# Retention in a four-layer language model tower: the next pair's work placed between a pair's masks, with a second query buffer

## The reference, cut to what matters

```
q, k, v = x @ W_Q, x @ W_K, x @ W_V              # each (B, T, H, 16)
scores  = (q . k) / 4 * decay                    # causal, decay = gamma_h ** (t - s)
out     = scores @ v
normed  = (out - mean) / sqrt(var + 1e-5) * weight + bias      # by head
y       = silu(x @ W_G + normed) @ W_O
```

## Time and profile before

| | us |
|---|---|
| median of three runs | 2263.53 |
| the profiled execution | 2263.48 |
| its span, first to last instruction | 2261.7 |
| retention, four pairs: first scores to the last residual sum (389.74 to 573.12) | 183.4 |
| TensorE busy over the span | 1845.4 |
| VectorE busy over the span | 1746.0 |
| ScalarE busy over the span | 1316.9 |

### The profile page before, as it was taken

The page is one execution under the profiler, slowest core; times in us unless marked ns, Lnnn a source line. Parts: engine busy times, 40 slices in busy tenths (PEclk is TensorE's granted clock), DMA queues, the critical chain, the costliest instruction groups (busy, mean ns, idle before and its releaser), DMA issues. The chain is left out here.

```text
span 2261.7 us, 31852 instructions
## 1 busy us (share of the span) xinstructions
PE 1845.4 (82%) x11804; PEld 950.2 (42%) x11804; DVE 1746.0 (77%) x4911; ACT 1316.9 (58%) x1459; POOL 328.4 (15%) x392
## 2 busy tenths in 40 slices
PE   6999998988766678999899998889999889755930
PEld 3566655766421123344333443333443364333520
DVE  3676557667777789999999999999999889785532
ACT  1222222231226999999999999999999822110410
POOL 6000111010343000000000000000000000057256
PEclk9898998787778899999999999999999999877965
DMA  5501000000001100000000000000000000031732
GB/s 167 182 1 38 18 1 14 1 1 1 1 0 36 66 1 1 1 1 1 1 1 1 1 1 1 1 1 1 1 1 1 1 1 1 0 140 52 229 106 75
DMA packets 39658, 64.98 MB, mean 29 GB/s; under 512 B 7744, under 2 KB 27728, under 8 KB 38736
## 3 DMA queue, kind: packets, MB, share of 16 engines
q1 hardware_dynamic: 30768, 39.86, 5.3%
q0 software_dynamic: 8736, 23.10, 3.3%
HBM read 37.77 MB, written 23.07 MB: 27 GB/s over the span
## 5 line engine op out<-in xcount | busy, mean ns | idle before, releaser
L1944 ACT ACTIVATE KM<-KM 128x2048 f32<-128x2048 f32 x290 | 539.0, 1909 | 8.0 <-DVE KM L1767 8.0
L1767 DVE TENSOR_SCALAR KM<-big 128x512 f32<-128x512 f32 x1160 | 479.5, 479 | 39.3 <-PE bank L2082 33.6
L2082 PE MATMUL bank<-KM,w_a_wa 128*32 128x512 f32 x2736 | 379.1, 628 | 92.4 <-ACT KM L1944 71.0
L191 POOL TENSOR_TENSOR nrstd<-nrstd,minus_half 128x4 f32<-128x4 f32 (+1 forms) x80 | 82.3, 1049 | 1735.7 <-DVE nrstd L168 1735.5
L1944 ACT ACTIVATE aa_args<-aa_args 128x2048 f32<-128x2048 f32 x142 | 266.1, 1910 | 1.5 <-DVE aa_args L1767 1.5
L1767 DVE TENSOR_SCALAR aa_args<-big 128x512 f32<-128x512 f32 x568 | 235.5, 479 | 13.5 <-PE bank L2082 12.9
L2082 PE MATMUL bank<-aa_args,w_a_wa 128*32 128x512 f32 x1360 | 188.8, 629 | 40.7 <-ACT aa_args L1944 26.8
L2082 PEld LDWEIGHTS bank<-KM,w_a_wa 128*32 128x32 f32 x2736 | 54.7, 109 | 243.0 <-ACT KM L1944 140.7
L1941 ACT ACTIVATE KM<-big 128x512 f32<-128x512 f32 x208 | 132.9, 718 | 0.0
L2048 PE MATMUL bank_pair<-XT,rf_wgu 128*128 128x256 f32 x320 | 88.3, 398 | 0.8 <-DVE ST L1839 0.8
L2054 PE MATMUL bank_pair<-XT,rf_wgu 128*128 128x256 f32 x320 | 88.2, 398 | 0.0
(11 more groups left out here) (451 smaller groups left out, 3300.6 us busy)
## 6 DMA issues: line engine op xcount, KB each, us to landing
queues<-zeros SPq DMA_DIRECT2D x1, 8192.0 KB, 24.0
KM<-queues SPq DMA_DIRECT2D x32, 256.0 KB, 3.7
results<-KM POOLq DMA_DIRECT2D x32, 256.0 KB, 3.1
w<-in_w SPq DMA_DIRECT2D x1, 4096.0 KB, 13.1
mf_tv<-in_task_W SPq DMA_DIRECT2D x1, 2048.0 KB, 9.3
la_v<-in_task_W SPq DMA_DIRECT2D x1, 2048.0 KB, 8.0
big<-XN SPq DMA_DIRECT2D x8, 256.0 KB, 2.7
rf_wgu<-in_wgu SPq DMA_DIRECT2D x1, 2048.0 KB, 8.2
```

The source lines that it names most:

```text
L191: self.nc.gpsimd.tensor_tensor(self.m.nrstd[s][:, 0:self.tiles], self.m.nrstd[s][:, 0:self.tiles], self.m.minus_half[:, 0:self.tiles], ALU ...
L1767: last = nc.vector.tensor_scalar(ARG(n, step)[:, cc, :], KU[:, i * T:(i + 1) * T], q, None, ALU.add)
L1944: last = nc.scalar.activation(ARG(n, step), ARG(n, step), ACT.Tanh)
L2082: last = nc.tensor.matmul(m.bank[g][32 * cc:32 * cc + 32, :], w["a_wa"][:, 30 - 2 * k:62 - 2 * k], ARG(n, step)[:, cc, :], start=k == 0, s ...
```

## The change: what it does

It rewrites the hand-written order of the lists for the four pairs. No matrix product and no elementwise operation is dropped.

- Two query buffers: pair i uses `QPS[i % 2]`, in `m.KM`.
- VectorE: `masks` come unit by unit. Between them stand the tanh product (`activated`) and the residual sum (`residual`) of the pair before, the gate's norm (`gate_stats`, `gate_scale`), the scaling for the next pair (`vector_scale`) and, behind the last mask, `front` of the next pair. The statistics of the norm come one pair earlier (`front_norm`). States and products alternate at a pair's end.
- TensorE: `gate_inputs`, `project` of the pair before, `attend` of the first sequence, `turn` and `turn_b` stand between the scores; `keys` stands ahead of `attend` of the second sequence.
- ScalarE: `gates` is first, `values` stands between the root and the tanh, and two 128x1 activations on a spare tile ask for the tables of the root and of the tanh.
- In the fourth pair `project` and `residual` of the third come ahead of the first `columns`.

```
-    QP = [m.KM[s][:, 0:2, :].rearrange("p b t -> p (b t)") for s in S]
+    QPS = [[m.KM[s][:, 2 - 2 * k:4 - 2 * k, :].rearrange("p b t -> p (b t)") for s in S] for k in range(2)]
+    QP = lambda i, s: QPS[i % 2][s]
...
@@ VectorE @@
             front(0)
-            states(0)
+            front_norm(1)
+            for c in range(NS):
+                states(0, c)
             for i in range(PAIRS):
...
+                masks(i, (0,))
+                if i:
+                    activated(i - 1)
+                if last:
+                    residual(i - 1)
...
+                else:
+                    masks(i, (1, 2))
+                    if i:
+                        residual(i - 1)
+                    masks(i, (3,))
+                    if i:
+                        gate_stats(i - 1)
+                    masks(i, (4,))
+                    norm.vector_scale(dve, i, norm.pair(i + 1), XN)
+                    masks(i, (5,))
+                    if i:
+                        gate_scale(i - 1)
+                    masks(i, (6, 7))
+                    front(i + 1)
+                    if i + 2 < PAIRS:
+                        front_norm(i + 2)
...
+                    states(i + 1, 0)
+                    normed(i, 0)
+                    states(i + 1, 1)
+                    normed(i, 1)
+                    states(i + 1, 2)
+                    gated(i)
@@ ScalarE @@
+                squares(i, 1)
+                nc.scalar.activation(ready_for[:, 0:1], m.zeros[:, 0:1], ACT.Sqrt)
                 act.wait_ge(var_sb.sem, var_sb.at(i, 2))
                 nc.scalar.activation(gvar[:, :], gvar[:, :], ACT.Sqrt).then_inc(root.sem, 1)
+                if i + 1 < PAIRS:
+                    values(i + 1)
+                nc.scalar.activation(ready_for[:, 1:2], m.zeros[:, 0:1], ACT.Tanh)
@@ TensorE @@
+                scores(i, (0,))
+                if i:
+                    gate_inputs(i)
+                if i + 1 == PAIRS:
+                    project(i - 1)
+                    columns(0, 0)
...
+                else:
+                    scores(i, (1, 2))
+                    if i:
+                        project(i - 1)
+                    scores(i, (3, 4))
+                    attend(i, (0,))
+                    scores(i, (5, 6))
+                    turn(i + 1)
+                    scores(i, (7,))
+                    if i:
+                        turn_b(i - 1)
+                    variances(i, (0,))
+                    keys(i + 1)
+                    attend(i, (1,))
+                    if i:
+                        logits(i - 1)
+                    variances(i, (1,))
+                    values(i + 1)
+                    widen(i, (0,))
+                    states(i + 1, 0)
+                    widen(i, (1,))
+                    states(i + 1, 1)
+                    states(i + 1, 2)
```

More of the change, by code:

```diff
@@ L1036, in _ @@
             norm.gpsimd(pool, 2)
-            for i in range(1, PAIRS):
-                norm_b.gpsimd(pool, i)
+            norm_b.gpsimd(pool, 1)
+            norm_b.gpsimd(pool, 2)
+            norm_b.gpsimd(pool, 3)
             for n in range(HALVES * TILES):
@@ L1170, in _ @@
             front(0)
-            states(0)
+            front_norm(1)
+            for c in range(NS):
+                states(0, c)
             for i in range(PAIRS):
[L1173 to L1179, removed]
+                last = i + 1 == PAIRS
+                masks(i, (0,))
[3 more added lines that the diff above has]
+                    residual(i - 1)
                     for u in range(len(UNITS)):
-                        masks(i, (u,))
+                        if u:
+                            masks(i, (u,))
                         for part in range(6):
@@ L1433, in variances, with widen @@
                     last.then_inc(var_ps.sem, 1)
-            def widen(i):
-                for s in S:
+            def widen(i, ss=S):
+                for s in ss:
                     pe.wait_ge(spread.sem, spread.at(i, s + 1))
@@ L1521, in _ @@
             values(0)
-            states(0)
+            for c in range(NS):
+                states(0, c)
             for i in range(PAIRS):
-                nxt = i + 1 < PAIRS
-                if nxt:
-                    scores(i, range(len(UNITS)))
-                    attend(i)
-                    turn(i + 1)
-                else:
-                    for u in range(len(UNITS)):
+                scores(i, (0,))
[4 more added lines that the diff above has]
+                    columns(0, 0)
+                    for u in range(1, len(UNITS)):
                         scores(i, (u,))
@@ L1535, in _ @@
                     attend(i, (1,))
-                variances(i)
-                if nxt and i:
-                    turn_b(i - 1)
-                if nxt:
+                    variances(i)
+                    widen(i)
+                    project(i)
+                else:
+                    scores(i, (1, 2))
[9 more added lines that the diff above has]
+                    variances(i, (0,))
                     keys(i + 1)
-                widen(i)
-                if nxt and i:
-                    logits(i - 1)
-                if nxt:
+                    attend(i, (1,))
+                    if i:
+                        logits(i - 1)
+                    variances(i, (1,))
                     values(i + 1)
-                project(i)
-                if nxt:
-                    states(i + 1)
+                    widen(i, (0,))
[3 more added lines that the diff above has]
+                    states(i + 1, 2)
             turn_b(PAIRS - 2)
```

139 lines of the change are left out of this document (78 added, 61 removed).

## The result

| | before | changed |
|---|---|---|
| median, same chip (6 runs each) | 2264.23 us | 2241.49 us |
| lowest to highest | 2260.45 to 2265.09 | 2235.13 to 2249.42 |
| the profiled execution, and its span | 2263.48, 2261.7 | 2240.6, 2238.7 |

The ratio is 0.9904 with a 95% interval of 0.9883 to 0.9925: faster by 1.0%, some 22 us.

What follows compares the result with a forecast made beforehand. It took middle pairs to be bound by a 13 us mask stretch paced by slow scores, then a chain without overlap. Pairs at −7.2, −7.6, −6.8 and +5.0 sum to −16.6: 2263.5 to 2246.9 us, range 2239 to 2258.

Steps and rivals of the forecast that it cites:

- VectorE's 19.2: Middle pair: masks, tanh product, residual sum, gate statistics and scalings take VectorE 19.2 us, from t = 2.0 to 21.2.
- TensorE's tail: Middle pair behind the last mask: TensorE work 11.1 us, ScalarE copies 1.5, then 2.7 to the next scores; period 36.5.
- The allowance: Middle pair: 1.5 us for one stretch at half clock on the path, raising the period from 36.5 to 38.0.
- First pair: First of four pairs: earlier attend raises the clock sooner; 34.4 us, 35.4 with clock allowance, against 42.6, so −7.2.
- Fourth pair: Last pair: balance rounds wait for the third pair's residual sum, first reduction at 7.7 instead of 2.7, so +5.0 us.
- Tables: ScalarE's table requests ahead of root and tanh: worth 0, as the root's table load already starts early; no drain.
- Unit 0 alone: Scores: units 0 and 1 no longer run together, 1.1 us more TensorE time a pair; 0 taken, 1.1 the bound.
- Nothing behind the block: Code behind the block: claimed not to change, so it adds nothing to the −16.6 us.
- Rival 1: Half clock lasts through the masks: middle pair 44.3 us, first 38.4, sum −1.0, 2262.5 us, no difference; chance 0.10.
- Rival 2: Half clock also holds the tail, pair becomes TensorE-bound: middle pair 52 us, sum +17, 2281 us, slower; chance 0.05.
- Rival 3: Some 20 TensorE-VectorE hand-overs a pair: ten idles of 0.4 make middle pairs 42 us, −6, 2257.5 us; chance 0.12.
- a sign of being wrong: Forecast wrong if VectorE waits over 3 us inside masks, middle clock is at most 0.8, or fourth pair grows over 7.

Runs made afterwards that it cites:

- two kernels with other clocks: Kernel before with a full-row filler matmul per unit of scores in the first three pairs: 128x256, ratio 1.0055; 128x64, ratio 1.0076.
- the two orders with a clock of 1.00: Changed kernel with values ahead of variances and logits, 2241.54 us; the same with the last pair's mask 1 brought forward, 2244.57 us.
- the first pair's 41.1: First pair of the changed kernel with the gate's norm, its turn and logits moved behind the masks; ratio 0.9960 to the kernel before.

## Why the prediction was right

- **Bound, and the cut.** That a middle pair was two stretches without overlap, and that the change puts them side by side, holds: 30.4 us behind the masks became 16.6, and the same 30.4 stood in two kernels with other clocks. What the forecast left to its rivals is how much the new order depends on the clock: with one attend moved or one projection put back, the clock fell as well, and most or all of the gain went.
- **VectorE's 19.2.** Predicted t = 21.2 for the last mask, measured 21.0 (second pair, 443.1) and 20.3 (third: it waits for no scores, the second 0.67).
- **TensorE's tail.** 11.1 + 1.5 + 2.7 = 15.3, and 1.5 for one stretch at half clock, 16.8: measured 16.6 in the third pair, and the half-clock stretch is there to be seen, the values at 3.51 instead of 1.95. The allowance was the right size. For the last copies the prediction has 1.5 where its own rows give 1.2, and 1.2 is what they took (492.79 to 493.96). At full clock it had 36.5 for the period; the two orders with a clock of 1.00 took 35.5.
- **First pair** −7.2, measured −7.8, and this agreement is luck. The prediction's 34.4 does not come out of its terms: 18.8 and "the same tail without logits", 15.3 − 1.9, give 32.2, and 33.2 with the 1.0 for the clock, which would have been −9.4. The masks ended at t = 19.4, and the tail took 15.5, since TensorE stood idle for 1.35 (until 414.50) for ScalarE's squares, about where the logits would have been. And the pair depends on the clock by 3.2 us between two executions.
- **Fourth pair** +5.0, measured +5.3, with the first reduction at t = 7.0 against 7.7: 0.7 less there, and the untraced 1.0 more elsewhere.
- **Tables** 0, shown. **Unit 0 alone** 0: not tested by itself, but in the third pair VectorE waited for no scores at all. (Four pieces of work stand between the first and the last scores there; `turn_b` comes behind the last.)
- **Nothing behind the block**: I had no term for untouched code, and in the two profiled executions it ran 4.7 us shorter at a higher clock (2.6 ahead of the block, 2.4 behind it, +0.3 elsewhere), while the pairs gave −18.3 against −16.6. These two make the 6.4 between the forecast and the traces (5.4 between the medians and the forecast). In the second execution of the changed kernel the pairs gave −22.2 and the block began 3.4 later than before, for much the same time. So the split between pairs and untouched code is not a property of the change.
- **Rival 1** (half clock through the masks) was not tested as it stands. With the attend out, the clock was at 0.50 in the second half of the masks, and they still ended at t = 20.3. But with an attend at half clock among them VectorE waited 3.14 for scores in the changed kernel's first pair and 2.02 and 1.69 in the third pair of the kernel with the projection at the end. I had walked the lists with every TensorE item at half clock, projection and attend included; these rows neither confirm nor refute its 44.3.
- **Rival 2** (half clock in the tail) did not come in full, but it is the one with teeth: 2.3 of the moved attend's cost, 1.6 in the changed kernel's own values, and much of the first pair's 41.1 above.
- **Rival 3**, hand-overs: in the middle pairs VectorE waited under 1 us among the masks. In the first it waited 3.14, over the 3 us that the prediction named as a sign of being wrong, but behind a half clock and not in hand-overs.

## What to carry to other kernels

Look for the chain behind a loop that no other engine overlaps, and measure it from the last instruction in front of it to the next round. Here its length told what the change could cut; the engines' busy shares and their clock did not. When TensorE comes close to being the bound, a wait on it can cost about twice its length: the waits of 1.52, 2.06 and 2.49 us above each had a stretch at 1.2 GHz behind them that cost 1.4 to 1.7 more. It is no rule: behind the wait of 1.83 TensorE was at full clock, a wait of 1.26 was followed by the half clock in one pair and not in the next, and the clock also fell where TensorE had not waited at all. And moving VectorE's work out of the way gave nothing where it opened a wait elsewhere.

## What was unexpected in the hardware

- A TensorE that is busy for all of its time can lose the clock: with 128x64 fillers among scores of 32 rows it fell from 0.99 to 0.50 while busy 2.00 of 2 us, and with 128x256 fillers it stayed at 1.00 for a pair.
- Gaps of 1.26 and 2.18 us, or of 1.52, were followed by half clock (2.08 for a unit instead of 1.13, 3.39 instead of 1.96). In the changed kernel the same gap of 1.26 was followed by an attend at 3.57 in the second pair and at 1.95 in the third, where the clock fell only later, at about 489, after more than 10 us in which TensorE was busy throughout.
- The same kernel's first pair took 34.86 in one execution and 31.64 in another, at granted clocks of 0.81 and 0.95.
